# Causal attention on one core: query scores in pairs of PSUM banks, maxima in six instructions, values in three batches

## What is computed

```python
k = (x @ Wk).reshape(B, H, T, hs)      # B 32, H 6, T 1024, hs 16
q = (x @ Wq).reshape(B, H, T, hs)
v = (x @ Wv).reshape(B, H, T, hs)
wei = jnp.einsum('bhtd,bhsd->bhts', q, k) * scale
wei = jnp.where(mask, wei, -jnp.inf)
wei = jax.nn.softmax(wei, axis=-1)
out = jnp.einsum('bhts,bhsd->bhtd', wei, v).reshape(B, T, C)
```

## Time and profile before

| | us |
|---|---|
| median of three runs | 2903.25 |
| lowest and highest run | 2900.68, 2903.61 |
| span of the profiled execution | 2901.5 |
| attention stage, first query matmul to last output copy | 1008.7 to 2423.6 |

### The profile page before, as it was taken

One profiled execution on the slowest core, in us unless ns is written; L12 is line 12 of the kernel. 1 busy time (PEld: TensorE's weight loads), 2 busy tenths in 40 slices (PEclk: granted clock), 3 DMA queues, 4 the chain that ended last, 5 costly groups with the idle time before them and its releaser, 6 DMA issues. The chain is left out here.

```text
span 2901.5 us, 86028 instructions
## 1 busy us (share of the span) xinstructions
PE 2730.6 (94%) x28924; PEld 1685.7 (58%) x29306; DVE 2300.3 (79%) x4585; ACT 2020.8 (70%) x3943; POOL 1153.0 (40%) x1999
## 2 busy tenths in 40 slices
PE   4999999999999499999999999999999997899996
PEld 2555555555554266666666666666666664455553
DVE  3577676676765499999999999999999994678997
ACT  2677777777776267777777777777777774577775
POOL 1144443444434434444444444444444441224445
PEclk9999999999999699999999999999999998999998
DMA  1113223232332466666666666666666663334555
GB/s 34 44 55 115 90 100 114 76 114 85 105 114 85 128 118 119 116 118 118 118 118 118 118 118 118 118 117 117 117 117 117 118 117 86 99 105 132 147 142 154
DMA packets 923408, 316.04 MB, mean 109 GB/s; under 512 B 848785, under 2 KB 906418, under 8 KB 923314
## 3 DMA queue, kind: packets, MB, share of 16 engines
q1 hardware_dynamic: 921970, 313.59, 47.8%
q10 hardware_dynamic: 1344, 1.18, 0.1%
HBM read 113.35 MB, written 99.88 MB: 73 GB/s over the span
## 5 line engine op out<-in xcount | busy, mean ns | idle before, releaser
L982 DVE TENSOR_REDUCE at_unit_max<-at_ps_queries 128x1 f32<-128x512 f32 (+4 forms) x2304 | 1135.9, 550 | 86.0 <-PE at_ps_queries L853 83.5
L928 ACT ACTIVATE at_probs<-at_ps_keys 128x512 f32<-128x512 f32 x1344 | 743.3, 603 | 388.9 <-PE at_ps_keys L868 384.5
L853 PE MATMUL at_ps_queries<-at_turned 96*128 96x128 bf16 (+3 forms) x3456 | 635.1, 275 | 30.6 <-DMA at_turned<-at_spread 29.4
L868 PE MATMUL at_ps_keys<-at_turned 128*128 128x128 bf16 x3453 | 648.4, 275 | 13.3 <-ACT at_probs L928 1.7
L803 POOL TENSOR_TENSOR at_v<-at_stacks,at_one 128x128 f32<-128x128 f32 x192 | 76.7, 399 | 818.5 <-DMA at_stacks<-qkv_rows 818.5
L888 PE MATMUL at_ps_values<-at_probs,at_v 128*32 128x128 f32 x10752 | 373.4, 276 | 6.5 <-ACT at_probs L928 6.5
L868 PEld LDWEIGHTS at_ps_keys<-at_turned 128*128 128x128 bf16 x3456 | 238.0, 97 | 239.5 <-ACT at_probs L928 88.3
L853 PEld LDWEIGHTS at_ps_queries<-at_turned 96*128 96x128 bf16 x3456 | 289.7, 98 | 122.0 <-DMA at_turned<-at_spread 31.3
L888 PEld LDWEIGHTS at_ps_values<-at_probs,at_v 128*32 128x32 f32 x10752 | 269.5, 109 | 120.6 <-ACT at_diag_probs L928 70.2
L928 ACT ACTIVATE at_diag_probs<-at_ps_keys 128x512 f32<-128x512 f32 x384 | 208.7, 595 | 8.5 <-PE at_ps_keys L868 5.6
L822 POOL TENSOR_SCALAR_AFFINE_SELECT at_diag_probs<-at_diag_probs 128x1024 f32<-128x1024 f32 x192 | 210.3, 1095 | 0.0
(11 more groups left out here) (214 smaller groups left out, 4967.4 us busy)
## 6 DMA issues: line engine op xcount, KB each, us to landing
qkv_rows<-cb_packed SPq DMA_DIRECT2D x32, 1536.0 KB, 8.3
at_stacks<-qkv_rows SPq DMA_DIRECT2D x192, 256.0 KB, 3.3
cb_x<-in_x_dram SPq DMA_DIRECT2D x32, 384.0 KB, 3.7
cb_x_again<-in_x_dram SPq DMA_DIRECT2D x32, 384.0 KB, 4.5
x_after_conv<-cb_x SPq DMA_DIRECT2D x32, 384.0 KB, 5.0
attention_rows<-at_att SPq DMA_DIRECT2D x384, 32.0 KB, 2.2
ff_att_rows<-attention_rows SPq DMA_DIRECT2D x32, 384.0 KB, 4.5
ff_x<-x_after_conv SPq DMA_DIRECT2D x128, 96.0 KB, 2.4
```

Source lines behind the costliest of these rows:

```text
L853: mm = pe.matmul(pq[:, u % QBANKS, c0:c0 + n], QT[0:STACK, slot, qb * P:(qb + 1) * P], KT[0:STACK, slot, k0:k0 + n], start=(c0 == 0), stop ...
L868: mm = pe.matmul(pk[:, bank_k, c0:c0 + n * P], KT[:, slot, kb * P:(kb + 1) * P], QT[:, slot, q0 * P:(q0 + n) * P], start=(c0 == 0), stop=True,
L928: act.activation(probs, pk[:, (slot * NU + k) % KBANKS, :], ACT.Exp, scale=scale).then_inc(S["probs"], 1)
L982: dve.tensor_reduce(peaks, scores, AX.X, ALU.max).then_inc(S["unit_max"], 1)
```

## The change

Query scores: the four banks become two pairs (`QPAIRS`), and twelve units become five, each filling a pair. Unit 0 has all eight diagonal blocks with two masks, units 1 and 2 the 512-column rows of query blocks 4, 5 and 6, 7, unit 3 the blocks 3 and 1 beside 7 and 5, unit 4 the blocks 2 and 6. They stand at the steps 0, 2, 3, 5, 7. A unit waits for the maxima of the unit two before. DVE takes the maxima in six instructions with two or eight results each (`QMAXIMA`) in place of twelve. DVE's division of the output moves from before the last query unit to behind the joined maximum. The maximum's two parts move from DVE to POOL, at the start of POOL's pass. Values: two batches of five and four units, at steps 0 and 4, become three of three units, at steps 7 (v = 0, 1, 2), 1 (v = 3, 4, 5) and 4 (v = 6, 7, 8). The diff, cut to its core:

```diff
-    BATCHES = {4: (0, 1, 2, 3, 4), 8: (5, 6, 7, 8)}
-    QBANKS, KBANKS = 4, 2
+    BATCHES = {2: (0, 1, 2), 5: (3, 4, 5), 8: (6, 7, 8)}
+    QPAIRS, KBANKS = 2, 2
...
-    QUNITS = [[(1, 0, P)], [(2, 0, 2 * P)], QDIAG[0], [(4, 0, BANK)], [(5, 0, BANK)], [(3, 0, 3 * P)], [(6, 0, BANK)],
-              [(5, BANK, P)], QDIAG[1], [(7, BANK, 3 * P)], [(6, BANK, 2 * P)], [(7, 0, BANK)]]
+    QUNITS = [QDIAG, [[(4, 0, BANK)], [(5, 0, BANK)]], [[(6, 0, BANK)], [(7, 0, BANK)]],
+              [[(3, 0, 3 * P), (1, 0, P)], [(7, BANK, 3 * P), (5, BANK, P)]], [[(2, 0, 2 * P), (6, BANK, 2 * P)]]]
+    QMAXIMA = [[(0, 8, 1, 2, P, 0, P)], [(4, 6, 1, 0, BANK, 0, BANK)], [(6, 8, 1, 0, BANK, 0, BANK)],
+               [(3, 8, 4, 1, BANK, 0, 3 * P), (1, 6, 4, 1, BANK, 3 * P, P)], [(2, 7, 4, 1, 2 * P, 0, 2 * P)]]
...
-    QSTEP = [1, 2, 2, 3, 4, 4, 5, 6, 6, 7, 7, 8]
+    QSTEP = [0, 2, 3, 5, 7]
...
-    OUT_QUNIT = 11
...
-        pq = pb("queries", [P, QBANKS, BANK])
+        pq = pb("queries", [P, QPAIRS, 2 * BANK])
...
+                    if on(3):
+                        q = (r - 3) % SLOTS % 2
+                        pool.wait_ge(S["head_max"], i - 2)
+                        _above(pool.wait_ge, S["max_turned"], i - 4)
+                        pool.tensor_tensor(MP[:, q, 0:TILES], NM[:, :], ONE[:, :, 0].broadcast_to([P, TILES]), ALU.mult
+                                           ).then_inc(S["max_high"], 1)
+                        pool.wait_ge(S["max_high"], i - 2)
+                        pool.tensor_tensor(MP[:, q, TILES:2 * TILES], NM[:, :], MP[:, q, 0:TILES],
+                                           ALU.subtract).then_inc(S["max_parts"], 1)
...
-                    _above(pe.wait_ge, S["unit_max"], NQ * h + u - QBANKS + 1)
...
+                    before = MAXDONE[u - QPAIRS] if u >= QPAIRS else MAXDONE[u - QPAIRS + NQ] - NMAX
+                    _above(pe.wait_ge, S["unit_max"], NMAX * h + before)
+                    pair = pq[:, (NQ * r + u) % QPAIRS, :]
+                    for b, blocks in enumerate(QUNITS[u]):
...
+                    if on(2):
+                        for u, maxima in enumerate(QMAXIMA):
                             dve.wait_ge(S["q_scores"], NQ * (i - 2) + u + 1)
...
+                            for first, last, every, part, pitch, c0, n in maxima:
...
+                                dve.tensor_reduce(MX[:, r % 2, first:last:every, part], scores, AX.X, ALU.max
+                                                  ).then_inc(S["unit_max"], 1)
...
-                        dve.tensor_copy(MP[:, r % 2, 0:TILES], NM[:, :]).then_inc(S["max_high"], 1)
-                        dve.wait_ge(S["max_high"], i - 1)
-                        dve.tensor_tensor(MP[:, r % 2, TILES:2 * TILES], NM[:, :], MP[:, r % 2, 0:TILES],
-                                          ALU.subtract).then_inc(S["max_parts"], 1)
```

More of the change, by code:

```diff
@@ L697, in causal_attention @@
     SLOTS = 6
-    BATCHES = {4: (0, 1, 2, 3, 4), 8: (5, 6, 7, 8)}
-    QBANKS, KBANKS = 4, 2
+    BATCHES = {2: (0, 1, 2), 5: (3, 4, 5), 8: (6, 7, 8)}
+    QPAIRS, KBANKS = 2, 2
     QDIAG = [[(qb, qb * P, P) for qb in range(g, g + HALF)] for g in (0, HALF)]
-    QUNITS = [[(1, 0, P)], [(2, 0, 2 * P)], QDIAG[0], [(4, 0, BANK)], [(5, 0, BANK)], [(3, 0, 3 * P)], [(6, 0, BANK)],
-              [(5, BANK, P)], QDIAG[1], [(7, BANK, 3 * P)], [(6, BANK, 2 * P)], [(7, 0, BANK)]]
+    QUNITS = [QDIAG, [[(4, 0, BANK)], [(5, 0, BANK)]], [[(6, 0, BANK)], [(7, 0, BANK)]],
+              [[(3, 0, 3 * P), (1, 0, P)], [(7, BANK, 3 * P), (5, BANK, P)]], [[(2, 0, 2 * P), (6, BANK, 2 * P)]]]
+    QMAXIMA = [[(0, 8, 1, 2, P, 0, P)], [(4, 6, 1, 0, BANK, 0, BANK)], [(6, 8, 1, 0, BANK, 0, BANK)],
+               [(3, 8, 4, 1, BANK, 0, 3 * P), (1, 6, 4, 1, BANK, 3 * P, P)], [(2, 7, 4, 1, 2 * P, 0, 2 * P)]]
     NQ = len(QUNITS)
-    QSTEP = [1, 2, 2, 3, 4, 4, 5, 6, 6, 7, 7, 8]
+    QSTEP = [0, 2, 3, 5, 7]
+    NMAX = sum(len(m) for m in QMAXIMA)
+    MAXDONE = [sum(len(m) for m in QMAXIMA[:u + 1]) for u in range(NQ)]
     LAG = 11
@@ L849, in query_scores @@
                         pe.wait_ge(turned_in[slot], _dmas(lap, r, 2, SLOTS))
-                    _above(pe.wait_ge, S["unit_max"], NQ * h + u - QBANKS + 1)
[L851 to L858, removed]
+                    before = MAXDONE[u - QPAIRS] if u >= QPAIRS else MAXDONE[u - QPAIRS + NQ] - NMAX
+                    _above(pe.wait_ge, S["unit_max"], NMAX * h + before)
+                    pair = pq[:, (NQ * r + u) % QPAIRS, :]
+                    for b, blocks in enumerate(QUNITS[u]):
+                        c0 = b * BANK
+                        for qb, k0, n in blocks:
+                            mm = pe.matmul(pair[:, c0:c0 + n], QT[0:STACK, slot, qb * P:(qb + 1) * P],
+                                           KT[0:STACK, slot, k0:k0 + n], start=(c0 == b * BANK), stop=True,
+                                           skip_group_check=True)
+                            c0 += n
+                        if len(blocks) == HALF:
+                            mm = pe.matmul(pair[:, b * BANK:(b + 1) * BANK], w["ident_bf"][:, :],
+                                           w["mask_queries"][:, :], start=False, stop=True, skip_group_check=True)
                     mm.then_inc(S["q_scores"], 1)
@@ L964, in body @@
                 def body(i, r, lap, on):
[L965 to L974, removed]
-                            dve.wait_ge(S["q_scores"], NQ * (i - 2) + u + 1)
[L976 to L984, removed]
+                    if on(2):
+                        for u, maxima in enumerate(QMAXIMA):
+                            dve.wait_ge(S["q_scores"], NQ * (i - 2) + u + 1)
+                            pair = pq[:, (NQ * r + u) % QPAIRS, :]
+                            for first, last, every, part, pitch, c0, n in maxima:
+                                count = len(range(first, last, every))
+                                scores = pair[:, 0:count * pitch].rearrange("p (t n) -> p t n", n=pitch)
+                                scores = scores[:, :, c0:c0 + n]
+                                dve.tensor_reduce(MX[:, r % 2, first:last:every, part], scores, AX.X, ALU.max
+                                                  ).then_inc(S["unit_max"], 1)
+                        dve.wait_ge(S["unit_max"], NMAX * (i - 1))
                         _above(dve.wait_ge, S["max_parts"], i - 2)
```

10 lines of the change are left out of this document (8 added, 2 removed).

## The result

The changed kernel takes 3121.61 us (median of four runs, 3120.23 to 3123.44), the kernel before beside it 2901.97 us: a ratio of 1.0756, 95% interval 1.0741 to 1.0772. It is 220 us slower. I had forecast 3150 us. The profiled execution has a span of 3121.7 us.

The account below looks back on a forecast made before the run. PE in its written order was taken to bound the kernel. Third batch 0.23, step 1 0.42, steps 6 and 7 0.70, less 0.04 made +1.31 us a head, over 190 heads 249 us: 3150 us, range 3040 to 3200.

Parts of the forecast that it names:

- What bounds: Attention stage: PE in its written order sets the time at 7.18 us an undisturbed head; DVE follows with 0.40 us spare.
- Third batch, +0.23: PE's added values batch: holes of 0.10 us before and 0.13 after, 0.23 us a head.
- (1): Rival: only the third batch costs, as exponentials run further ahead and PE's waits vanish; 2936 us, chance 0.07.
- (2): Rival: batch holes are waits for exponentials, so a third batch is free and smaller ones help; 2858 us, chance 0.03.
- Step 1, +0.42: Values batch 3, 4, 5: its third unit waits for exponential 7, 0.42 us a head.
- Steps 6 and 7, +0.70: Keys 4 wait 0.29 us for exponential 2's bank, values 0, 1, 2 wait 0.41 for the output copy.
- the same walk: Step-by-step timing of one head on PE in the new order, giving 8.53 us against 7.18.
- Small holes, -0.04: Small holes in PE's old order that go away, 0.04 us a head less.
- the lap's 0.11 us a head: Extra time per head over an undisturbed one, averaged over a six-head lap; predicted to stay at 0.11 us.
- "Two pairs of banks ... Price 0": Pairs replacing four single query-score banks: DVE frees them in time, price 0, up to 0.3 us a head if late.
- the 0.6 to 0.9: DVE time saved per head by six fewer row-maxima instructions, in us; predicted gain on the path 0.
- Rival (4): A pair of banks is late too, 0.3 us more a head: 3207 us, chance 0.04.

Follow-up runs that it names:

- e6: Changed kernel with the maximum's two parts taken back from POOL to DVE: 3121.23 us, ratio 1.0754.
- e3: Kernel before with its values batch of four units cut into two of two, at steps 3 and 4: 2940.90 us, ratio 1.0134.
- e5: Changed kernel with ACT's output copy at step 4 in place of 5: 3088.36 us, ratio 1.0633.
- e7: Changed kernel with the two values batches of before, pairs reordered and each bank filled at a step of its own: 2890.32 us, ratio 0.9951.
- e1: Changed kernel with the two values batches of before, five and four units: 3067.21 us, ratio 1.0568.
- e9: Changed kernel, three values batches kept, with pairs reordered and filled one bank at a time over more steps: 2988.12 us, ratio 1.0297.

## Why the prediction was right, point by point

**What bounds.** PE in its written order sets the time, DVE follows: held. The changed kernel's waits have no row of PE for a maximum or its parts, and e6 shows 2 us of DVE more in a lap costing nothing.

**Third batch, +0.23.** By e3 0.20 to 0.21 us a head. The estimate holds, and so does the reading that the holes are no waits; rivals (1) and (2) rested on the opposite or on vanishing waits.

**Step 1, +0.42.** Measured 0.33. The mis-sized term is the time from an exponential's end to the values matmul, which I put at 0.16 us. Here exponential 7 ends at 1671.70, and the batch's last unit starts 0.35 us (0.22 + 0.13) before the keys at 1672.11, so at 1671.76: 0.06 us. The 0.16 came from a misread row: I took the key matmul at 1507.86 to wait for its bank, 0.14 us after an exponential's end. Weight loads of the kernel before show what stands in front of it:

```profile
1507.58 0.10 PEld L857 LDWEIGHTS at_ps_queries<-mask_queries,ident_bf 128*128 128x128 bf16 x1
1507.76 0.10 PEld L868 LDWEIGHTS at_ps_keys<-at_turned 128*128 128x128 bf16 x1
```

That is the mask of a diagonal query unit. Its matmul has no record, as nearly all masks of that trace; behind the four blocks it runs from about 1507.63 to 1507.86. So the keys there came without a hole, and the 0.06 us that I counted before them was none.

**Steps 6 and 7, +0.70.** Measured 0.20 for keys 4 and 0.47 for the output copy: 0.67. Keys 4 start 0.06 us after their exponential, not 0.14, which takes 0.29 to 0.21. The output copy's end to the values is 0.14, close to my 0.16; but PE is at that batch 0.08 us earlier than I walked, since keys 4 were, so the wait is 0.47 and not 0.41. With these the same walk has 0.33 + 0.21 + 0.47 = 1.01 us of waiting in place of 1.12, a head of 8.38 us: measured 8.36. That two chains end at one point is nearly so: with the copy moved, the batch waits 0.28 us for exponential 4 (e5), and 0.20 of the 0.47 comes back.

**Small holes, -0.04.** 0.21 + 0.33 + 0.67 is 1.21, an undisturbed head grew by 1.18 (7.18 to 8.36), so 0.03 of old holes went, close to the estimate. What I had kept, the lap's 0.11 us a head, became 0.07 (8.43 less 8.36). That makes 1.14 us a head; my 1.31 gave 3150.

**What was wrong is whose cost it is.** "Two pairs of banks ... Price 0" holds for the pairs as buffers (e7), but no term of mine is for the places of the query scores. I checked only whether DVE frees a pair in time, and never asked what the missing query work at steps 1, 4, 6 and 8 uncovers. The wait of keys 4, which I entered in one term with the batch at step 7, belongs to those places: e1 has it with the batches of before. The total came out since the walk had all of the new order in it; the list of terms would have told a reader to undo the batches, and that returns 54 of 220 us (e1).

**DVE.** I expected 5.4 to 5.7 us a head, and DVE busy 65% to 70%; it is 6.15 (36.88 in six heads), 73%. Moving the parts of the maximum away saved 0.34 us a head (38.92 less 36.88 in six heads, e6), near my 0.4; the fewer reductions did not save the 0.6 to 0.9. Mean durations fell as I worked out (twelve of 550 ns, now six of 954, 0.88 us less), but busy time of the reductions only by 0.45 us a head (1135.9 to 1050.2 for 192), and DVE's as a whole by 0.21 beside the parts. Most of an instruction's fixed 154 ns had overlapped with its neighbours. That reading is argued, no run varied it; it has no part in the time.

**Chances.** The forecast's own mechanism came, inside its range. Rival (4), a pair that is late, showed in no run; in e9 a pair comes just in time.

## What to carry to other kernels

Where one engine works in a written order through several jobs, each step has two uses: its own work, and cover for what another engine is just doing. Before regrouping any work, even work that waits for nothing, list for every pair of dependent steps what stands between them, and compare it with the length of the chain (here 0.43 + 0.60 + 0.06 us over two banks); then walk the whole new order rather than pricing edits one by one, since such prices don't add (165 and 163 us gave 220). And when a walk gets the total, take one part back at a time before believing its list of terms.

## What the runs showed of the hardware

Going from full-width matmuls to four narrow ones side by side and back costs PE about 0.20 us, also where the data is old (e3). The fp32 matmuls of full width that turn the output go in and out without such a hole: in e7 the two stand at 1540.65 right behind keys at 1540.44 and take 0.22 us in all up to the next keys, less than the two holes of a batch (0.10 and 0.13) alone. A matmul that waits for an exponential starts 0.06 us after its end (keys 4 in the changed kernel, keys 5 and 6 in e1), the first values matmul 0.14 us after the output copy's. Two reductions of 512 columns from PSUM take 683 ns each; one of 1,024 over two banks takes 1,221:

```profile
L989 DVE TENSOR_REDUCE at_unit_max<-at_ps_queries 128x2 f32<-128x1024 f32 x238 | 280.6, 1221 | 107.8 <-PE at_ps_queries L868 107.8
```
